# A sparse-attention block on one core: compressed scores cut to the visible blocks, their mask added by VectorE

## The reference, cut to what matters

```
sc = einsum('bhsd,bhnd->bhsn', q4, ck4) * SCALE            # 64 compressed blocks of 16 tokens
comp_mask = (arange(nb) + 1) * CS <= arange(s)[:, None]    # a block is seen once it lies wholly in the past
out_comp = masked_softmax(sc, comp_mask) @ cv4
imp = sc.mean(axis=(1, 2)); top_idx = top_k(imp, 2)        # unmasked means choose two blocks
out_sel = masked_softmax(q4 @ sel_k * SCALE, causal) @ sel_v    # 8 tokens of each chosen block: 16 keys
out_win = masked_softmax(q4 @ k4 * SCALE, last 128 tokens) @ v4
out = g0 * out_comp + g1 * out_sel + g2 * out_win
```

## Time and profile before

| what | us |
|---|---|
| median of the runs | 2564.87 |
| the profiled execution | 2562.29 |
| its span, first to last instruction | 2560.4 |
| TensorE busy (matmul) | 2241.7 |
| VectorE busy | 1747.1 |
| ScalarE busy | 1446.9 |
| GpSimd busy | 889.9 |

### The profile page before, as it was taken

The page is one execution under the profiler, slowest core; times in us unless marked ns, Lnnn a source line. Parts: engine busy times, 40 slices in busy tenths (PEclk is TensorE's granted clock), DMA queues, the critical chain, the costliest instruction groups (busy, mean ns, idle before and its releaser), DMA issues.

```text
span 2560.4 us, 55188 instructions
## 1 busy us (share of the span) xinstructions
PE 2241.7 (88%) x18184; PEld 1447.0 (57%) x18184; DVE 1747.1 (68%) x4612; ACT 1446.9 (57%) x4829; POOL 889.9 (35%) x780
## 2 busy tenths in 40 slices
PE   3888999899998999989998999989999899977676
PEld 0756666556664666556664666646665566644443
DVE  3466777578776777667786677757777578765654
ACT  1245666556654666556664566646665466645553
POOL 0435333333334333243332433343332433333221
PEclk9998999999998999989999999989999899998888
DMA  6010001100011000110002000110001100020000
GB/s 213 21 34 14 26 26 34 55 26 22 26 43 47 18 26 26 41 48 26 26 22 68 22 26 18 51 39 26 26 26 38 51 26 22 22 66 17 13 18 13
DMA packets 48844, 90.10 MB, mean 35 GB/s; under 512 B 6760, under 2 KB 6760, under 8 KB 48544
## 3 DMA queue, kind: packets, MB, share of 16 engines
q1 hardware_dynamic: 39328, 69.51, 8.9%
q10 hardware_dynamic: 9216, 16.78, 1.8%
HBM read 69.45 MB, written 16.83 MB: 34 GB/s over the span
## 4 chain that ended last, share of the span: by engine, by line
issue 56%; POOL 28%; PE 8%; ACT 3%; DVE 3%; DMA 1%; POOLq 1%; SPq 0%; DVEq 0%; ACTq 0%
POOL csp L1211 6%; POOL css L1203 4%; POOL xc L1238 3%; POOL h_lo L1231 3%; POOL ra L1243 3%; POOL kr L1195 3%; POOL ra L1195 3%; POOL wo_s L1219 1%; ACT pw L982 1%; PE ps_m L690 1%; POOL wbt_s L1225 1%; PE ps_o L622 1%; PE ps_m L495 1%; PE ps_m L497 1%; PE ps_m L496 1%
## 5 line engine op out<-in xcount | busy, mean ns | idle before, releaser
L982 ACT ACTIVATE pw<-ps_s,wmax 128x128 f32<-128x128 f32 x1024 | 358.6, 378 | 147.3 <-DVE wmax L1455 147.3
L495 PE MATMUL ps_m<-w_hi,h_hi 128*128 128x512 f32 x768 | 352.8, 459 | 75.6 <-DVE rbf L1422 31.5
L992 ACT ACTIVATE pw<-pw,wden 128x128 f32<-128x128 f32 x1024 | 313.2, 388 | 124.3 <-DVE wden L1465 124.3
L1015 ACT ACTIVATE pT<-ps_s 128x512 f32<-128x512 f32 x240 | 142.4, 593 | 306.2 <-PE ps_s L616 222.7
L497 PE MATMUL ps_m<-w_hi,h_lo 128*128 128x512 f32 x768 | 308.3, 401 | 0.0
L496 PE MATMUL ps_m<-w_lo,h_hi 128*128 128x512 f32 x768 | 307.7, 401 | 0.0
L690 PE MATMUL ps_m<-wbt_s,h2T 128*128 128x512 f32 x512 | 259.7, 613 | 0.4 <-ACT zs L998 0.4
L655 PE MATMUL ps_m<-wo_s,aT 128*128 128x512 f32 x512 | 252.5, 616 | 0.9 <-ACT aT L1019 0.8
L1231 POOL TENSOR_TENSOR h_lo<-hT,h_hi 128x512 fp32r<-128x512 f32 x57 | 72.2, 1267 | 514.1 <-ACT h_hi L933 514.1
L495 PEld LDWEIGHTS ps_m<-w_hi,h_hi 128*128 128x128 f32 x768 | 147.7, 192 | 176.6 <-issue 90.1
L1211 POOL TENSOR_TENSOR csp<-csp,cden 128x256 f32<-128x256 f32 (+1 forms) x128 | 169.7, 1345 | 221.4 <-DVE cden L1504 221.4
(11 more groups left out here) (189 smaller groups left out, 4614.0 us busy)
## 6 DMA issues: line engine op xcount, KB each, us to landing
xa<-x_in SPq DMA_DIRECT2D x65, 256.0 KB, 2.7
xc<-x_in SPq DMA_DIRECT2D x64, 256.0 KB, 2.7
out<-t ACTq DMA_DIRECT2D x64, 256.0 KB, 2.0
wo_s<-wo_in SPq DMA_DIRECT2D x8, 1024.0 KB, 6.1
wbt_s<-wbt_in SPq DMA_DIRECT2D x8, 1024.0 KB
gbc<-gate_rows SPq DMA_DIRECT2D x24, 256.0 KB, 5.2
pw<-wmod_in SPq DMA_DIRECT2D x3, 1024.0 KB, 5.6
pT<-wmod_in SPq DMA_DIRECT2D x3, 1024.0 KB, 5.2
```

The lines of the kernel that those rows point to most:

```text
L495: pe_.matmul(ps[:], h_hi[:, c, :], w_hi[:, col, c, :], start=(c == 0), stop=False)
L982: ins = act.activation(pw[:, hw, :], ps_w[:, j, i, 1, :], ACT.Exp, bias=wmax[:, hw:hw + 1], accum_out=wden[:, 0, hw:hw + 1])
L992: act.activation(pw[:, hw, :], pw[:, hw, :], ACT.Copy, scale=wden[:, 2, hw:hw + 1]).then_inc(wn_ok, 1)
```

## The change

TensorE no longer writes the mask. It computes the scores of tile t over n = 16 + 8(t + 1) keys only, and each of these matmuls starts its own accumulation. ScalarE's `cs_copy` is gone; in its place stands `cs_mask` on VectorE, two additions of PSUM and the mask into `css`, each over two banks (8 heads x n elements). It waits for the scores and for the former tile's exponentials, and frees the banks. In VectorE's order it stands just ahead of `cs_max`. The mask tile becomes f32. The maxima, subtraction, exponentials, sums, normalisation and transposes run over the seen blocks only, and the values contract over 64 + 8(t + 1) rows. The order of all other work is the same on every engine.

```
+def blocks_seen(t):
+    return (t + 1) * (P // CB)
...
-        csmask = sb("csmask", [P, NT, CS], BF16)
+        csmask = sb("csmask", [P, NT, CS])
...
-        parts = ((0, NSEL), (NSEL, CS))
+        def parts(t):
+            return (0, NSEL), (NSEL, NSEL + blocks_seen(t))
...
-                for j in range(4):
-                    pe_.matmul(ps_s[:, j, 0:4 * CS].rearrange("p (c n) -> p c n", c=4), ident_b[:, :],
-                               csmask[:, t, :].unsqueeze(1).broadcast_to([P, 4, CS]),
-                               start=True, stop=False, skip_group_check=True)
+                n = NSEL + blocks_seen(t)
...
-                        mm = pe_.matmul(ps_s[:, j, c * CS:(c + 1) * CS], qT[rows, c, t * P:(t + 1) * P], csk[rows, c, :],
-                                        start=False, stop=True, skip_group_check=True)
+                        mm = pe_.matmul(ps_s[:, j, c * CS:c * CS + n], qT[rows, c, t * P:(t + 1) * P], csk[rows, c, 0:n],
+                                        start=True, stop=True, skip_group_check=True)
...
+                rows = P - NB + blocks_seen(t)
...
-                    mm = pe_.transpose(dst[:, j, :], csp[:, NC * j + g, :], ident)
+                    mm = pe_.transpose(dst[0:rows, j, :], csp[:, NC * j + g, 0:rows], ident)
...
-                    mm = pe_.matmul(ps_o[HD * j:HD * j + HD, c, :], src[:, cols], probs[:, j, :], start=start, stop=stop,
+                    mm = pe_.matmul(ps_o[HD * j:HD * j + HD, c, :], src[0:rows, cols], probs[0:rows, j, :], start=start, stop=stop,
...
-            def cs_copy(b, t):
-                T = NT * b + t
-                n = QUADS * b + quad(t, "cs")
-                act.wait_ge(s_full, n + 2)
-                act.wait_ge(cs_exp, 2 * T + 1)
-                for p in range(2):
-                    ins = act.activation(css[:, 8 * p:8 * p + 8, :].rearrange("p (j c) n -> p j (c n)", j=2),
-                                         ps_s[:, 2 * p:2 * p + 2, 0:4 * CS], ACT.Copy)
-                ins.then_inc(s_done, 1)
...
-                act.activation(csp[:, :, P - NB:P], css[:, :, NSEL:CS], ACT.Exp).then_inc(cs_exp, 1)
+                n = blocks_seen(t)
+                act.activation(csp[:, :, P - NB:P - NB + n], css[:, :, NSEL:NSEL + n], ACT.Exp).then_inc(cs_exp, 1)
...
+            def cs_mask(b, t):
+                T = NT * b + t
+                n = NSEL + blocks_seen(t)
+                dve.wait_ge(s_full, QUADS * b + quad(t, "cs") + 2)
+                dve.wait_ge(cs_exp, 2 * T + 1)
+                mask = csmask[:, t, 0:n].unsqueeze(1).unsqueeze(1).broadcast_to([P, 2, 4, n])
+                for p in range(2):
+                    ins = dve.tensor_tensor(css[:, 8 * p:8 * p + 8, 0:n].rearrange("p (j c) n -> p j c n", j=2),
+                                            ps_s[:, 2 * p:2 * p + 2, 0:4 * CS].rearrange("p j (c n) -> p j c n", c=4)[:, :, :, 0:n],
+                                            mask, ALU.add)
+                ins.then_inc(s_done, 1)
...
+                cs_mask(b, s)
                 cs_max(b, s)
```

More of the change, by code:

```diff
@@ L614, in transpose_cs, with add_values @@
                 dst = spare_t if spare_bank else ps_t
+                rows = P - NB + blocks_seen(t)
                 for j in range(4):
-                    mm = pe_.transpose(dst[:, j, :], csp[:, NC * j + g, :], ident)
+                    mm = pe_.transpose(dst[0:rows, j, :], csp[:, NC * j + g, 0:rows], ident)
                 mm.then_inc(tc_full, 1)
-            def add_values(c, src, probs, start, stop):
+            def add_values(c, src, probs, start, stop, rows=P):
                 for j in range(4):
                     cols = slice(P * c + HD * j, P * c + HD * j + HD)
-                    mm = pe_.matmul(ps_o[HD * j:HD * j + HD, c, :], src[:, cols], probs[:, j, :], start=start, stop=stop,
+                    mm = pe_.matmul(ps_o[HD * j:HD * j + HD, c, :], src[0:rows, cols], probs[0:rows, j, :], start=start, stop=stop,
                                     skip_group_check=True)
@@ L643, in cs_values @@
                 pe_.wait_ge(tc_done, n + 2)
-                add_values(g, csv, pT_cs[:, g % 2], False, True).then_inc(pvc_done, 1)
+                add_values(g, csv, pT_cs[:, g % 2], False, True, P - NB + blocks_seen(t)).then_inc(pvc_done, 1)
             def output(seg, b, t, chunks=range(NC)):
@@ L1014, in probs_copy @@
                     act.wait_ge(pvc_done, n)
-                act.activation(pT_cs[:, g % 2], (spare_t if t_spare(t, g) else ps_t)[:], ACT.Copy).then_inc(tc_done, 1)
+                rows = P - NB + blocks_seen(t)
+                act.activation(pT_cs[0:rows, g % 2], (spare_t if t_spare(t, g) else ps_t)[0:rows], ACT.Copy).then_inc(tc_done, 1)
             def copy_out(b, t):
@@ L1051, in first_slot @@
                 copy_out(b, 0)
-                cs_copy(b, 1)
                 if a:
@@ L1076, in slot @@
                 Ta = NT * ba + t
-                cs_copy(b, s)
                 if a:
@@ L1130, in turn @@
                     copy_zT(seg, b, t)
-                cs_copy(ba, 0)
                 if c2:
@@ L1200, in cs_subtract @@
                 gp.wait_ge(cs_ok, CS_STEPS * T + 4)
-                for w, (lo, hi) in enumerate(parts):
+                for w, (lo, hi) in enumerate(parts(t)):
                     v = css[:, :, lo:hi]
@@ L1208, in cs_normalise @@
                 gp.wait_ge(cs_ok, CS_STEPS * T + CS_STEPS + 1)
-                for lo, n, w in ((0, NSEL, 2), (P - NB, NB, 3)):
+                for lo, n, w in ((0, NSEL, 2), (P - NB, blocks_seen(t), 3)):
                     v = csp[:, :, lo:lo + n]
@@ L1495, in cs_factor @@
                 dve.wait_ge(cs_exp, 2 * T + 3)
-                for w, (lo, n) in enumerate(((0, NSEL), (P - NB, NB))):
+                for w, (lo, n) in enumerate(((0, NSEL), (P - NB, blocks_seen(t)))):
                     dve.tensor_reduce(cden[:, w, :], csp[:, :, lo:lo + n], AX.X, ALU.add).then_inc(cs_ok, 1)
@@ L1636, in first_slot @@
                     gates_soft(seg, b, t, Ta, 0)
+                cs_mask(b, 1)
                 cs_max(b, 1)
@@ L1721, in turn @@
                 mod_copy((ba + 1) % B, mod_a, 0, moda_ok)
+                cs_mask(ba, 0)
                 cs_max(ba, 0)
```

## The result

The changed kernel takes 2502.01 us (median of 4 runs, 2496.73 to 2503.68) against 2563.86 (4 runs, 2562.22 to 2566.15) for the kernel before on the same chip: ratio 0.9755, 95% interval 0.9738 to 0.9772. In the experiments' first group it was 2500.12 (5 runs), ratio 0.9757, interval 0.9744 to 0.977. 2508 had been forecast, between 2488 and 2535. The profiled spans are 2560.4 and 2500.7, 59.7 us apart.

The account below looks back on a forecast made before the run. TensorE sets the loop's pace; the last batch is a chain of waits. Loop slots 36.5, turns and first slots 15.5, last batch 5.5: 57.5 us off 2562.29, 2504.8; medians run 2.6 higher, 2507.4, said 2508, range 2488 to 2535.

Parts of the forecast that it names:

- TensorE, the mask: Four mask matmuls per tile ahead of the scores go: 0.65 us per tile, 64 tiles, 41.6 us where TensorE sets the pace.
- Fewer columns, narrower transposes: TensorE's scores and csp transposes: zero taken; rivals 25 us more gain (chance 0.07) or 26 us lost (0.10).
- VectorE's adds: Two mask adds per tile out of PSUM: 0.48 to 0.82 us each, pairs 0.88 to 1.55 us, for s = 2 to 7.
- The upper bound of 2.08 times: Highest price allowed for VectorE's broadcast mask adds against the plain PSUM row; pairs would take 1.9 to 3.3 us.
- The slower rival: VectorE's chain between scores and window_max becomes the bound, adds at 2.08 times the row: 2573 us, chance 0.06.
- The new wait: cs_mask on VectorE waits for scores; window_max still 1.73 to 0.40 us earlier, loop slots gaining 5.2 us a batch, 36.5 in seven.
- Slots s = 2 to 6: Loop slots gain 1.1, 1.1, 1.05, 0.9 and 0.67 us by the earlier window_max, the first three capped by the window scores.
- Turn and first slot: final in turn 1.8 us earlier, first-slot scores 0.65 earlier: 1.95 us a batch taken (1.3 to 2.7), eight times, 15.5 us.
- All 1.8 us come through, or 0.65: At the loop's jump: final's whole gain survives, or 0.65 us if the restart hangs on the weight transfer TensorE's end starts.
- the second cause: Restart behind the loop's jump hangs on the weight transfer that TensorE's end starts; only 0.65 us come through.
- Last batch: Slots s = 2 to 7, where the chain is the length, gain 5.5 us by window_max, capped by the window scores.
- Only TensorE's own time comes back: Rival: gaps reopen elsewhere in the slot, 0.65 us for all slots but s = 7: 39.6 us, 2525 us, chance 0.20.

Follow-up runs that it names:

- the experiments' first group: The changed kernel again, unaltered, as yardstick beside the kernel before (2563.93 us): 2500.12 us, ratio 0.9757.
- wide loads: Changed kernel with transposes of the compressed probabilities, the copies behind them and the values over all 128 rows: 2498.92 us, ratio 0.9749.
- wide maxima: Changed kernel with VectorE's maxima over all 64 blocks for every tile, one memset added: 2506.41 us, ratio 0.9771.
- wide sums: Changed kernel with VectorE's sums of the compressed probabilities over all 64 blocks for every tile: 2516.56 us, ratio 0.9814.
- the kernel with the mask alone: Changed kernel with the mask added by VectorE but every width left full (80 columns, 128 rows): 2548.37 us, ratio 0.9936.
- without the reload: Loop-end reload of the feed-forward's base and experts' matrices cut to 4 columns: 2501.07 us from the changed kernel, 2561.91 from the kernel before.
- wide scores: Changed kernel with the scores' matmuls over all 80 columns for every tile: 2499.55 us, ratio 0.9747.
- the late one: Changed kernel with the reload of both feed-forward matrices held until the next batch's first compressed exponentials are done: 2502.03 us, ratio 0.9754.

## Why the prediction was right, point by point

- **What bounds the kernel**: right. TensorE sets the pace in the loop with short gaps, and each gap is a hand-over from VectorE or ScalarE. The 1.15 us for Q's rotation were read from the weight queue's row; the matmuls themselves stood 0.74 us there, and 0.56 after.
- **TensorE, the mask**: 0.65 us a tile predicted; 0.56 between last product and scores.
- **Fewer columns, narrower transposes: zero**: right, shown by two kernels. That narrowed loads are not shorter was read from the 113-column row and is wrong (122 to 141 ns at 72 to 120 columns), but nothing hung on it. The Trainium skill ("TensorE: Matmul & The Clock Gate", Weight-path perf modes) keeps the fast weight load to types other than FP32. By that rule narrowing f32 loads costs nothing, and the runs agree: ratio 0.9749 with wide loads, 0.9757 with narrow ones.
- **VectorE's adds**: row by row right. The upper bound of 2.08 times was made real by the doubled adds: 2553.9 us, not 2573 and not slower than before. The slower rival's price was too high by 19 us. Against the kernel before its slots s = 2 to 7 lost 1.1 us a loop batch and not 2.0: s = 2, 3, 4 and 7 came out 0.1 to 0.6 better than priced (an early window_max only waits for its window scores there), s = 5 and 6 0.3 worse. The rest lies outside the loop batches: the first batch gained 2.5 us and the last 4.7, where each was to lose 1.
- **The new wait**: times of window_max right to 0.01 us from s = 4 on, but what it is worth was not. Counted from the scores' start of s = 4, window_max is 0.56 us earlier (4.42 before, 3.86 after) and the product behind Q's rotation only 0.23; the mask ahead of the scores, 0.65 by its rows, comes to both. What eats the rest stands in between, in the weights of the window branch (`window_weights`), before and after, and GpSimd's subtraction beside it after:

```profile
918.09 0.37 DVE L1465 TENSOR_SCALAR wden<-wden,gates 128x8 f32<-128x8 f32 x1
...
1190.96 0.70 DVE L1460 TENSOR_SCALAR wden<-wden,gates 128x8 f32<-128x8 f32 x1
1191.02 1.84 POOL L1198 TENSOR_TENSOR css<-css,cm 128x256 f32<-128x256 f32 x2
```

  Counted from the scores' starts (908.59 before, 1182.01 after) L1460 starts 0.55 us earlier but takes 0.33 longer. It takes 0.23 us where GpSimd does nothing, in all 14 profiles; before, it started late in the first of GpSimd's two subtractions (0.62 us), now ahead of it, and either way it ends 0.03 us after that one. So 0.22 are left. The kernel with wide maxima agrees: window_max is 0.40 us later in it, L1460 takes 0.37, and the product is 0.07 later. The prediction counted GpSimd as hidden in the loop and idle at the slot's start; that an earlier VectorE meets it further on was left out.
- **Slots s = 2 to 6**: 1.1, 1.1, 1.05, 0.9 and 0.67 predicted, 4.8 together; 1.34, 0.85, 1.27, 0.86 and 0.78 measured, 5.1. The sum hit, its parts not. At s = 4 the 1.27 are 0.56 of mask, 0.23 up to Q's product, 0.35 from there to the window values and 0.13 later. The 0.35 come from VectorE's narrower work in mid-slot, which the prediction left out: the sums account for 0.15 by the kernel with wide sums alone, the rest was not taken apart. s = 3 lacks 0.4 us since VectorE stands still 0.41 us ahead of a masked copy (L1471) there, an idle time that the profile puts down to issue; the kernel with the mask alone has the same 0.41 us there and also gains 0.4 less at s = 3 than at s = 4.
- **Turn and first slot**: the step that failed in part. 1.95 us a batch predicted; s = 0 and s = 1 gave 0.00 and 1.20, slot 7 with the turn 0.63, of which 0.40 was the slot's by the prediction: 1.4. final is 1.9 us earlier, as worked out. But before, the restart hung on VectorE's resuming (9.84 us, then window_max and h_lo); once that is earlier, ScalarE's is next (10.3), and behind it TensorE's. "All 1.8 us come through, or 0.65" was a choice between two causes where there are three in a row. For ScalarE the second cause is the one that the runs show: its last instruction before the jump, the store's issue, comes 3.98 us after the scores where it was 5.23, but it resumes at 10.5 us where it was 10.1 (means of six turns), as the transfer is issued 3.0 us after the scores in both; without the reload it resumes at 8.4, and at 9.4 in the kernel before. Beside the mask's own time 0.1 us came through (first products 13.77 us after the scores before and 13.63 after, means of six turns), and the projection behind it took back more: the granted clock comes back to the upper level 18.8 to 19.1 us after the scores, where it came back at 16.6 to 17.9. In the turn shown the second window scores take 1.67 us for it where they took 1.15, so the way to tile 1 is as long as before although its mask is gone. By the Trainium skill ("Runtime: NRT & Kernel Launch", Instruction fetch mechanics) a taken branch whose target isn't in the fetched pages fetches it before execution goes on; the prediction took from it that each delay starts at the engine's own jump. TensorE agrees (6.8 to 7.2 us after the scores without the transfer, 6.7 to 7.8 with it); that ScalarE resumes 2 us earlier without the transfer is more than that rule says.
- **Last batch**: 5.5 for its slots and 1.95 for its start predicted, 7.5; 8.5 measured. The sum hit, its parts not: slots s = 2 to 6 gave 7.9 us where 5.1 were predicted, s = 0 and s = 1 gave 1.96 and -0.39, and from the last tile's scores to the end 0.9 were lost.
- **Not foreseen**: the first batch gained 11.3 us, 3.8 of them on the way to tile 1. That way took 19.6 to 24.9 us over all profiles, and the granted clock explains only part of the spread: 24.92 us at 0.86 before, 21.08 at 0.92 and 21.90 at 0.84 in the two profiles of the changed kernel, and 19.56 at 1.00 with wide scores, where slot s = 1 then took 30.73. No run was made to settle why, and it stays open. So the nearness of the sum, 57.5 us forecast and 59.7 measured in the spans, is in part luck: the six loop batches gave 41.7 us where 42.9 were counted, the first 11.3 where 7.2, the last 8.5 where 7.5, and 1.9 of scatter in the start-up went off again.

The rival "Only TensorE's own time comes back" (2525) fell with the slots of 33.2 to 33.5 and the kernel with narrowing alone (2521.5 while the mask stayed on TensorE).

## What to carry to other kernels

When work moves from the engine that sets the pace to one that feeds it, the price on the feeder decides: the same move gave 16 us with full widths and 21 on top of the narrowing (8 of them in three slots whose cause is open), and doubling the adds took 54 back. Widths are worth cutting where a feeder runs without a pause (the sums gave about 16 us, though most of it not in the stretch that was named for it), not where the busy share falls most (GpSimd's 95 us gave nothing that can be measured). When an engine's work moves earlier, look for what runs beside it at its new place: 0.33 of 0.55 us went to GpSimd in that way. And ahead of counting a gain through a restart of several engines, list who resumes when: the second latest caps it.

## What the runs showed of the hardware

- A VectorE add from PSUM with a three-dimensional broadcast operand goes at the pace of a plain one: 820 ns at 640 elements, 481 at 320. Writing bf16 in place of f32 changes nothing (820 and 815).
- f32 weight loads for a transpose: 122, 120, 127, 128, 135, 137, 141 and 146 ns at 72, 80, 88, 96, 104, 112, 120 and 128 columns, but 174 ns for the 113 columns of the z transpose. Why was not tried.
- The two TENSOR_SCALAR operations shown above, on VectorE, end 0.02 to 0.04 us after a GpSimd operation when they start inside it: 0.70 us in place of 0.23 for 8 elements per partition beside the first subtraction, 1.07 in place of 0.18 for 32 beside h_lo (the doubled adds at s = 5). Over the 14 profiles the first of them started inside a GpSimd operation 920 times; 890 times it ended so, and 30 times it took its 0.23 us. The TENSOR_REDUCE that ran beside the same h_lo at s = 7 kept its 1.54 us.
- Behind the loop's jump ScalarE resumed 2 us and VectorE 1.3 us earlier when a 1 MB and a 0.23 MB transfer were not under way (in the kernel before 0.7 and 1.6); TensorE did not.
- In two of six turns without the reload, and in three of six with the late one, a way to tile 1 shortened by about 2 us was followed by a slot 1.7 to 3.2 us longer, in one of them shown with the granted clock at 0.66 for 10 us.
